# Small rows spread on chip by GpSimd, and the first loads dealt anew to two DMA queues

## The reference

```python
W = weights[condition]                       # (64, 64, 64)
y = einsum('bct,bcd->bdt', x, W)             # the mix: 64 x 1024 per sample
p = qweight.reshape(N, groups, 3)            # three words hold four values
v = [p0 & 63, (p0 >> 6) & 63, p1 & 63, p2 & 63]
w = (v - zero_point) * scale                 # one zero point and one scale per output column
out = x + einsum('bsk,nk->bsn', y, w) + bias
```

## Time and profile before

| | us |
|---|---|
| median of three runs | 286.27 |
| the profiled execution | 285.89 |
| its span, from the first instruction to the last | 283.9 |
| PE busy in the span | 277.6 |
| DVE busy | 186.1 |
| ACT busy | 83.9 |
| GpSimd busy | 95.4 |

### The profile page before, as it was taken

How to read it: one execution, slowest core, us unless ns; L and a number is a source line. 1 busy time by engine, 2 the same in 40 slices (tenths; PEclk the granted TensorE clock), 3 DMA queues, 4 the chain that set the end, 5 groups by cost and what they waited for, 6 DMA issues and landing times.

```text
span 283.9 us, 8490 instructions
## 1 busy us (share of the span) xinstructions
PE 277.6 (98%) x3307; PEld 231.8 (82%) x3307; DVE 186.1 (66%) x255; ACT 83.9 (30%) x169; POOL 95.4 (34%) x38
## 2 busy tenths in 40 slices
PE   8999999899999999999999999999999999999995
PEld 3888888788888888988888888888888888888885
DVE  3776886785566566865559555676667655595554
ACT  3786323342044300633017310443106330060000
POOL 0008602964430444314442444404443044430000
PEclk9999999999999999999999999999999999999999
DMA  7992571456114541345114551144413552101112
GB/s 278 398 306 81 161 240 65 152 159 230 74 74 157 160 179 66 115 163 195 74 74 124 167 208 74 74 155 157 154 70 117 166 195 95 74 37 74 74 74 74
DMA packets 20685, 39.48 MB, mean 139 GB/s; under 512 B 6850, under 2 KB 7106, under 8 KB 20674
## 3 DMA queue, kind: packets, MB, share of 16 engines
q1 hardware_dynamic: 19730, 36.96, 37.3%
q10 hardware_dynamic: 944, 2.38, 2.3%
HBM read 22.54 MB, written 16.78 MB: 138 GB/s over the span
## 4 chain that ended last, share of the span: by engine, by line
PE 96%; DMA 2%; issue 1%; ACT 1%; DVE 0%; SPq 0%
PE o_ps L286 71%; PE y_ps L286 12%; PE y_ps L255 10%; DMA w_sb<-in_L_cond_weights_dram 1%; PE o_ps L255 1%; PE o_ps L268 0%; DMA ids<-in_itok_B_dram 0%; PE o_ps L297 0%; ACT qT L436 0%; PE y_ps L268 0%; SPq L155 0%; PE y_ps L297 0%; ACT y_hi L420 0%; DVE o_sb L607 0%; DVE o_sb L609 0%
## 5 line engine op out<-in xcount | busy, mean ns | idle before, releaser
L286 PE MATMUL o_ps<-qT,y_hi 128*128 128x512 f32 (+1 forms) x448 | 171.6, 386 | 0.2 <-ACT qT L436 0.2
L286 PE MATMUL o_ps<-qT,y_lo 128*128 128x512 f32 (+1 forms) x448 | 171.2, 385 | 0.0
L627 POOL TENSOR_TENSOR resid<-x_sb,bias_bc 128x1024 f32<-128x1024 f32 x32 | 94.7, 2968 | 154.9 <-DVE o_sb L534 134.1
L286 PEld LDWEIGHTS o_ps<-qT,y_hi 128*128 128x128 f32 x448 | 83.6, 188 | 17.4 <-ACT qT L436 0.4
L286 PEld LDWEIGHTS o_ps<-qT,y_lo 128*128 128x128 f32 x448 | 83.6, 188 | 16.8
L526 DVE TENSOR_TENSOR o_sb<-o_ps,scale_bc 128x512 f32<-128x512 f32 x54 | 37.3, 692 | 75.6 <-PE o_ps L286 75.6
L420 ACT ACTIVATE y_hi<-y_ps 128x512 fp32r<-128x512 f32 x56 | 29.4, 610 | 99.2 <-PE y_ps L255 98.8
L534 DVE TENSOR_TENSOR o_sb<-o_sb,resid 128x512 f32<-128x512 f32 x63 | 51.5, 823 | 1.9
L411 ACT ACTIVATE junk<-x_sb 128x1024 bf16<-128x1024 f32 x32 | 33.9, 1058 | 60.7 <-DMA x_sb<-in_x_dram 60.7
L515 DVE SCALAR_TENSOR_TENSOR resid<-zs_bc,ysum,resid 128x1024 f32<-128x1024 f32 x32 | 42.5, 1329 | 0.0
L505 DVE TENSOR_TENSOR y_lo<-y_ps,y_hi 128x512 fp32r<-128x512 f32 x57 | 35.7, 684 | 6.6 <-ACT y_hi L420 6.6
(11 more groups left out here) (35 smaller groups left out, 64.0 us busy)
## 6 DMA issues: line engine op xcount, KB each, us to landing
x_sb<-in_x_dram SPq DMA_DIRECT2D x32, 512.0 KB, 3.3
out_dram<-o_sb SPq DMA_DIRECT2D x63, 256.0 KB, 2.1
q_raw<-in_L_ffn_qweight_dram ACTq DMA_DIRECT2D x6, 384.0 KB, 5.3
w_sb<-in_L_cond_weights_dram SPq DMA_DIRECT2D x63, 16.0 KB, 2.0
q_raw<-in_L_ffn_qweight_dram SPq DMA_DIRECT2D x2, 384.0 KB, 6.3
scale_bc<-_L_ffn_weight_scale_dram SPq DMA_DIRECT2D x1, 512.0 KB, 5.8
zs_bc<-n_weight_zero_point_dram SPq DMA_DIRECT2D x1, 512.0 KB, 5.9
bias_bc<-in_L_ffn_bias_dram SPq DMA_DIRECT2D x1, 512.0 KB, 6.6
```

Of the source, the lines that this page charges most:

```text
L286: last = nc.tensor.matmul(bank, part[:, slot, kt, :], qT[:, kt, col:col + width], start=(kt == 0 and part is y_hi), stop=(kt == KT - 1 and ...
L627: nc.gpsimd.tensor_tensor(resid[:, j % RING, :], x_sb[:, j % RING, :], bias_bc[:], ALU.add).then_inc(xbias_ready, 1)
```

## The change

The three rows are loaded once each, into one partition of a new tile `rows_sb`, 4 KB a row, and SP issues these loads ahead of those of tiles 2 and 3. GpSimd spreads each row over the 128 partitions (`partition_broadcast`), after the fourth block has been unpacked, and DVE's two waits and GpSimd's own are now for that. Among the first loads, ACT's queue takes both halves of tile 0's condition weights and x of tile 1; SP's queue takes block 2 of the packed weights.

```diff
-        def load_row(eng, dst, src, s):
-            eng.dma_start(dst, src.partition_broadcast(P)).then_inc(s, 16)
+        def load_row(eng, place, src, s):
+            eng.dma_start(rows_sb[0:1, place, :], src).then_inc(s, 16)
...
             sp.wait_ge(ids_loaded, 16)
-            load_w_half(sp, 0, 0, pick(sp, 0))
-            load_x(1, 0)
+            load_q(sp, 2)
             load_w(1, 0)
             for n in (4, 6):
                 load_q(sp, n)
+            load_row(sp, 0, scale.rearrange("n a -> a n"), scale_loaded)
+            load_row(sp, 1, zero.rearrange("n a -> a n"), zero_loaded)
+            load_row(sp, 2, bias.rearrange("(a n) -> a n", a=1), bias_loaded)
             for j in range(2, RING):
                 load_x(j, 0)
                 load_w(j, 0)
-            load_row(sp, scale_bc[:], scale.rearrange("n a -> (n a)"), scale_loaded)
-            load_row(sp, zs_bc[:], zero.rearrange("n a -> (n a)"), zero_loaded)
-            load_row(sp, bias_bc[:], bias, bias_loaded)
...
             act.wait_ge(ids_loaded, 16)
-            load_w_half(act, 0, 1, pick(act, 1))
-            for n in (2, 3, 5, 7):
+            for half in range(2):
+                load_w_half(act, 0, half, pick(act, half))
+            act.dma_start(x_sb[:, 1, :], x_rows[P:2 * P, :]).then_inc(x_loaded[1], 16)
+            for n in (3, 5, 7):
                 load_q(act, n)
...
-            dve.wait_ge(scale_loaded, 16)
+            dve.wait_ge(scale_spread, 1)
...
-            dve.wait_ge(zero_loaded, 16)
+            dve.wait_ge(zero_spread, 1)
...
+            pool.wait_ge(q_part, 3 * RING)
+            pool.wait_ge(scale_loaded, 16)
+            nc.gpsimd.partition_broadcast(scale_bc[:], rows_sb[0:1, 0, :]).then_inc(scale_spread, 1)
+            pool.wait_ge(zero_loaded, 16)
+            nc.gpsimd.partition_broadcast(zs_bc[:], rows_sb[0:1, 1, :]).then_inc(zero_spread, 1)
             pool.wait_ge(bias_loaded, 16)
+            nc.gpsimd.partition_broadcast(bias_bc[:], rows_sb[0:1, 2, :]).then_inc(bias_spread, 1)
             pool.wait_ge(q_part, 3 * NT)
+            pool.wait_ge(bias_spread, 1)
```

More of the change, by code:

```diff
@@ L69, in adaln_ffn @@
         ident = sb("ident", [P, P], BF16)
+        rows_sb = sb("rows_sb", [1, 3, N], F32)
         scale_bc = sb("scale_bc", [P, N], F32)
@@ L109, in adaln_ffn @@
         bias_loaded = sem("bias_loaded")
+        scale_spread = sem("scale_spread")
+        zero_spread = sem("zero_spread")
+        bias_spread = sem("bias_spread")
         blank_ready = sem("blank_ready")
```

## The result

The changed kernel takes 290.83 us, median of six runs (290.39 to 292.66), against 286.16 (285.71 to 287.05) for six of the kernel before on the same chip: 1.0168 times as long, 95% interval 1.0141 to 1.0195. That is 4.7 us slower, where 286.6 was forecast. The profiled execution has a span of 288.7 us, 4.8 more than before.

What follows compares the result with a forecast made beforehand. The prediction took TensorE, busy 277.6 of 283.9 us, as the bound. Weights +0.35 and block 3, rows and spreads with GpSimd 0 each, put on the 286.27 median, gave 286.6 us; range 285.9 to 288.2, 8 times in 10.

Steps and rivals of the forecast that it cites:

- the term of +0.35: Tile 0's weights: second half on ACT's queue lands at 6.85 instead of 6.51, first products 0.35 us later.
- rival A: Second weight half stuck on ACT's queue; decides from a landing of 7.36, up to +3.3 us, 289.6; chance 20 in 100.
- Block 3: Block 3's load on ACT's queue, with more data ahead of it: delay taken as 0 us, range 0 to 1.0.
- rival D: Block 3 late for PE's transposes: up to +1.35 us, 287.6; chance 5 in 100.
- Rows: Row loads of 4 KB each: DVE's 1.52 us wait for scale_bc goes, worth nothing at the end.
- Spreads: GpSimd's three row spreads: 1.2 us each, ending at 16.4 us, 12.6 to 20.7; 0 at the end.
- GpSimd's start: GpSimd's first add, behind the second MODIFY_POOL_CONFIG pair: starts at 16.4 to 24.8, latest 29.1 us; cost taken as nought.
- the limit of 28.2: Latest start of GpSimd's first add before PE waits for sums of x, with 6.1 us to spare.
- first products after 10.3 us: Sign of a wrong forecast at PE's first products, expected near 9.8 us; pointed to rival A.
- a wait for block 3: Sign of a wrong forecast: PE waits for block 3 at 11.5 us; pointed to rival D.

Runs made afterwards that it cites:

- e9: Changed kernel with SyncE held ahead of block 2 until both halves of tile 0's weights have landed; one run, 293.05 us.
- e3: Kernel before, with tile 0's weight halves and x of tile 1 on ACT's queue, block 2 on SyncE's, rows loaded as before; 288.44 us, ratio 1.009.
- e6: Kernel before, plus three full-row spreads on GpSimd into a spare tile that nobody reads; 289.31 us, ratio 1.0086.
- e8: Changed kernel with the first spread held until all eight blocks are unpacked instead of four; 295.26 us, ratio 1.0306.
- e11: Changed kernel with each row spread in four pieces of 256 columns, GpSimd waiting for each piece; 293.64 us, ratio 1.0252.
- e4: Changed kernel with the loads dealt to queues as before, rows still loaded once and spread by GpSimd; 288.94 us, ratio 1.0093.
- e7: Changed kernel with the first half of tile 0's weights back on SyncE's queue, ahead of block 2; 290.43 us, ratio 1.0139.
- e1: Kernel before, with both halves of tile 0's weights on ACT's queue, the rest as before; 290.94 us, ratio 1.0167.
- e10: Changed kernel with ScalarE held ahead of x of tile 1 until both halves of tile 0's weights have landed; one run, 293.53 us.
- e2: Kernel before, with block 2 on SyncE's queue and x of tile 1 on ACT's, weight halves still split; 286.8 us, ratio 1.0018.

## Why the prediction was wrong, step by step

- **Weights: the term of +0.35 was mis-sized, and this is rival A.** The issue times were right: 4.15 worked out, 4.12 measured. The landing was not: I took 2.7 us, shorter than any row of that stretch, on the argument that less stood ahead; it took 3.9. The nearest rows, 3.2 and 3.57, give a landing of 7.35 and 7.72 and would have put the likeliest case near A's threshold of 7.36. Measured: +1.55 at the first products instead of +0.35. Most of it is the later issue, which I had counted (4.12, against 2.94 for the later half before), and then took back by the short landing. e9 shows that the other queue holds the half. Against A I had said that only block 2 and x of tile 0 are there; SyncE's timeline after shows tile 1's halves too, issued beside the second half:

```profile
3.84 1.24 SPq L154 DMA_DIRECT2D w_sb<-in_L_cond_weights_dram  x2
```

  The Trainium skill (DMA: Bandwidth & Descriptors, section "Issuing engines are not separate DMA queues") has loads of all issuing engines interleave; by that rule the pair must share with SyncE's loads, and e9 agrees. I had weighed the rule only for the sum, and had not asked which loads would be under way beside the half.
- **Block 3: taken as 0, range to 1.0; this is rival D, and it was too small.** The term assumed a rate of 398 GB/s and 128 KB more ahead. Block 3's issue moved behind a pick, a half and x, from 4.1 to 5.37, and the rate fell to 212 to 270 GB/s. Its transposes are 2.88 us late, 1.33 beyond the weights. e3 holds both terms: +2.2 in all. How much of the delay is the later issue and how much the lower rate was not separated.
- **Rows: worth 0, right.** They landed in time (the first spread waited for VectorE, not for them), and the vanished wait for the scale bought nothing.
- **Spreads: the duration was near, a term was missing.** A spread took 1.3 to 1.6 us, where I had 1.2. I asked only when they end and what GpSimd does next, not what runs on VectorE meanwhile. Each unpack instruction that began 0.1 us or more inside a spread lasted until its end; that is 1.8 us at tile 0's second half (e6, e8, e11) and 2.7 to 2.8 in the total (e4, e6), with what the clock adds there. No rival of mine had it. The Trainium skill has the rule (SBUF — State Buffer, section "🔬 SBUF: two separate sides"): GpSimd and VectorE share a pair of SBUF ports, taken as an exclusive lock for a whole instruction by whichever starts first, a GpSimd instruction or one of VectorE's in a two-port mode or with two SBUF inputs (the latter only against a GpSimd instruction that reads SBUF). The traces agree: unpacking SBUF to SBUF is held (1.51 to 1.67 for 0.47), the copy from PSUM that begins inside e6's first spread is not (0.42), and in e8 the multiplication by the scale, with two SBUF inputs, takes 1.55 instead of 0.68 beside the second spread. In which mode the unpacking runs no run here shows. VectorE in e8, at the scale:

```profile
22.95 1.55 DVE L566 TENSOR_TENSOR o_sb<-o_sb,scale_bc 128x512 f32<-128x512 f32 x1 [1.48 <-POOL scale_bc L626]
```

- **GpSimd's start: right, with a margin that was not what I thought.** From the second MODIFY_POOL_CONFIG pair to the first add 7.3 us pass; the add starts at 25.97, inside 16.4 to 29.1 and ahead of 28.2, and costs nothing. But the limit of 28.2 looked only at PE's wait for sums of x. In e8 and e11, with adds at 32.77 and 31.58, VectorE's residual bites instead, and costs 4.4 and 3.3 us of PE's time.

Two of the signs that I had named for a wrong forecast were there: first products after 10.3 us (11.02, A) and a wait for block 3 (1.17, D).

## What to carry to other kernels

Where a load of a pair moves behind its twin, count its issue time, and give it at least the landing time of the nearest row; shorten it only with a row that shows it. Before work goes to an idle GpSimd, list what VectorE does SBUF to SBUF in that stretch and count a hold for each instruction that begins beside it. A thing that takes a wait from an engine off the critical path is worth nothing, and each part of the change is asked what it puts in front of the few loads that PE waits for.

## What the runs showed of the hardware

- Ahead of GpSimd's first add, behind a MODIFY_POOL_CONFIG pair, 6.7 to 7.6 us pass in which it waits for nothing that the profile shows (after, e4, e7 to e11), and 9.2 in e6, where three 512 KB rows are still being loaded in the first part of that stretch. The Trainium skill (GPSIMD Engine Reference, section "Instruction dispatch") gives about 6 for loading code there; the runs are above it.
- PE's clock fell to its lower level, 1.2 GHz, after some of the new waits, and a wait then costs more than its length. In e3, behind a wait of 2.1 us for the weights, the mix took 1.99 us instead of 1.16. Busy time of three stretches of e3, with the granted clock behind GpSimd's:

```profile
8.00:10.00 2.00, 2.00 (x66) 1.88 (x67) 0.30 (x2) 0.00 (x0) 0.00 (x0) 0.50 1.02 335
10.00:12.00 2.00, 1.58 (x16) 1.40 (x15) 1.29 (x3) 1.63 (x3) 0.00 (x0) 0.70 1.00 354
12.00:14.00 2.00, 1.95 (x16) 1.96 (x16) 1.50 (x4) 1.95 (x3) 0.00 (x0) 1.00 1.03 410
```

  In the profiled run of the changed kernel, with a wait of 1.9 us, the mix took 1.16 and the clock stayed at 1.00. e6's runs part as e4's do: 287.70 and 288.89 at a mean clock of 1.000, 289.31 to 289.98 at 0.994.
- Between 6.5 and 9.1 us the rate lay at 204 to 334 GB/s wherever tile 0's pair on ACT's queue and tile 1's on SyncE's were under way together (after, e1, e3, e8, e10, e11), and at 331 to 430 where tile 0's halves were dealt to both queues and tile 1's came later (before, e2, e4 to e7) or tile 0's had landed first (e9). In that stretch 278 of 436 packets are under 512 bytes after, and 38 of 346 before. What in these small loads slows the DMA was not tried.
